# Repeated columns in the gate products and row statistics carried from one stage into the next norm

## The reference

```
def _layernorm(x, axis=-1, eps=1e-05):
    m = jnp.mean(x, axis=axis, keepdims=True)
    v = jnp.var(x, axis=axis, keepdims=True)
    return (x - m) / jnp.sqrt(v + eps)

x = x + _L0_xattn_ref(_layernorm(x), ctx, ctx, ...)        # cross attention
x = x + _L0_attn_ref(_layernorm(x), ...)                   # token mixing
x = x + _L0_ffn_ref(_layernorm(x), gate_w, gate_b, ...)    # feed forward
...                                                        # layers 1 to 3 alike

gate_scores = jnp.einsum('bsd,de->bse', x, gate_w) + gate_b   # in the mixtures of experts
topk_val, topk_idx = lax.top_k(gate_scores, TOP_K)
```

## Time and profile before

| | us |
|---|---|
| median of 3 runs | 3088.95 |
| lowest, highest | 3085.35, 3089.32 |
| the profiled execution | 3088.85 |
| its span | 3087.0 |

### The profile page before, as it was taken

How to read it: one execution, slowest core, us unless ns; L and a number is a source line. 1 busy time by engine, 2 the same in 40 slices (tenths; PEclk the granted TensorE clock), 3 DMA queues, 4 the chain that set the end, 5 groups by cost and what they waited for, 6 DMA issues and landing times. The chain is left out here.

```text
span 3087.0 us, 102826 instructions
## 1 busy us (share of the span) xinstructions
PE 2499.1 (81%) x30020; PEld 1971.3 (64%) x30021; DVE 2154.2 (70%) x7789; ACT 1872.6 (61%) x5990; POOL 1776.9 (58%) x1942
## 2 busy tenths in 40 slices
PE   4964799489999879888999983489669999979571
PEld 2843687367777678766777761477547777758561
DVE  5978422478888868727888887632279999979525
ACT  3841444379999723347999975144358888847320
POOL 1832477367777664025777762057547777749271
PEclk9985899799999989889999996589889999989685
DMA  2002455311111030003333320135534544500132
GB/s 103 3 1 99 128 154 153 98 45 41 39 39 39 27 130 0 0 1 76 79 79 79 81 46 0 66 117 153 147 82 116 115 118 114 116 5 3 57 106 67
DMA packets 195910, 225.58 MB, mean 73 GB/s; under 512 B 24899, under 2 KB 166211, under 8 KB 194724
## 3 DMA queue, kind: packets, MB, share of 16 engines
q1 hardware_dynamic: 183076, 197.57, 24.3%
q0 software_dynamic: 12672, 25.98, 3.1%
HBM read 201.69 MB, written 21.76 MB: 72 GB/s over the span
## 5 line engine op out<-in xcount | busy, mean ns | idle before, releaser
L1803 POOL TENSOR_TENSOR sx<-sx,rs 128x1028 f32<-128x1028 f32 x384 | 731.3, 1904 | 280.4 <-DVE rs L1951 280.2
L1896 ACT ACTIVATE sx<-sx,nm 128x257 f32<-128x257 f32 x1536 | 771.1, 506 | 115.8 <-DVE nm L1939 115.8
L1939 DVE CUSTOM_DVE_ANT_0 sx<-bank,rows 128x257 f32<-128x257 f32 x1024 | 411.1, 421 | 50.8 <-PE bank L1886 48.5
L1606 ACT ACTIVATE hT<-bank,B 128x128 f32<-128x128 f32 x714 | 205.7, 367 | 279.6 <-PE bank L1574 277.8
L350 POOL TENSOR_TENSOR rstd<-var,nhalf 128x8 f32<-128x8 f32 x48 | 79.1, 1648 | 414.0 <-DVE var L381 414.0
L1896 ACT ACTIVATION_READ_ACCUMULATOR sx<-sx,nm 128x1 f32 x1536 | 290.9, 189 | 0.0
L1886 PE MATMUL bank<-kT,qb 32*128 32x257 f32 x3072 | 278.6, 428 | 0.0
L1958 DVE COPY pt<-bank 128x512 f32<-128x512 f32 x384 | 263.8, 687 | 2.0 <-PE bank L1821 1.7
L1821 PE MATMUL bank<-C,sx 128*128 128x128 f32 x1536 | 251.6, 286 | 2.8 <-POOL sx L1803 2.7
L1840 PEld LDWEIGHTS bank<-W,ct 128*128 128x128 f32 x1536 | 219.5, 192 | 52.1 <-DVE nm L1939 18.1
L1870 PE MATMUL bank<-pt,vs 128*32 128x128 f32 x6144 | 245.6, 277 | 4.7 <-ACT pt L1905 4.6
(11 more groups left out here) (391 smaller groups left out, 5629.4 us busy)
## 6 DMA issues: line engine op xcount, KB each, us to landing
ct<-in_ctxT SPq DMA_DIRECT2D x384, 128.5 KB
W<-in_L_w SPq DMA_DIRECT2D x159, 256.0 KB
rows<-rows_x SPq DMA_DIRECT2D x256, 128.5 KB
keep<-rows_keep SPq DMA_DIRECT2D x128, 128.5 KB
yg<-copy_outs SPq DMA_DIRECT2D x40, 256.0 KB
token_rows<-XN SPq DMA_DIRECT2D x24, 256.0 KB, 2.3
W<-in_L_w SPq DMA_DIRECT2D x1, 6144.0 KB, 16.9
W<-in_L_w SPq DMA_DIRECT2D x39, 128.0 KB
```

Source lines behind the costliest of these rows:

```text
L1803: pool.tensor_tensor(sx[:, j, :, 0:KEYS], sx[:, j, :, 0:KEYS], rs[:, j, :].unsqueeze(2).to_broadcast([P, 4, KEYS]), ALU.mult).then_inc(p_r ...
L1896: ins = act.activation(sx[:, j, h, 0:KEYS], sx[:, j, h, 0:KEYS], ACT.Exp, bias=nm[:, j, h:h + 1], scale=-1.0, accum_out=sm[:, j, h:h + 1])
L1939: dve.tensor_tensor_reduce(sx[:, j, h, 0:KEYS], B[h][:, 0:KEYS], add, -1.0, 3.0e38, ALU.add, ALU.min, nm[:, j, h:h + 1]).then_inc(s_summed ...
```

## The change

Four things are changed.

1. In the norms of the three mixtures the gate weights are streamed through each tile several times in one product: `gw` is broadcast along a new dimension of `wide` copies, so that a product has 128 columns (E = 8) or 120 (E = 24, and 96, 72, 48 at the end of a bank). The copies land in the columns behind the tile's own and are overwritten by the next tiles' products. Bank 4 now holds 20 tiles, bank 5 has 12.
2. Two cross attentions (x1, x2) and the butterfly's experts measure X's tiles as they add to them, in pairs: DVE `measure` (`bn_stats`), `gather_pair` (two `bn_aggr`), `keep_pair` (two `tensor_scalar`), POOL `root_pair` and `shift_pair`. 30 tiles are carried out of a cross attention, 28 out of the experts; the norm that follows (attn8's, rglru's, x2's) measures the rest.
3. Which engine normalises and which copies a group is given by strings, one letter a group. With carried statistics ACT and DVE alternate, DVE first (rglru: DVE alone). DVE now normalises with `rstd` and `nmr` and so waits for `stat_ready` in place of `rstd_ready`, in every norm. The norms of the two 16-head attentions give DVE one group in place of two, or seven to ACT in place of six.
4. The cross attentions' loop is written out for 16 slots before it loops, all three of them.

```
-                                h, j = t // (TILES // 2), t % (TILES // 2)
-                                pe.matmul(B[4 + h][:, j * E:(j + 1) * E], XNT[:, t * P:(t + 1) * P], gw, start=True, stop=True)
+                                h, j = (0, t) if t < GATE_TILES else (1, t - GATE_TILES)
+                                wide = min(P // E, 512 // E - j)
+                                pe.matmul(B[4 + h][:, j * E:(j + wide) * E].rearrange("p (r e) -> p r e", e=E), XNT[:, t * P:(t + 1) * P],
+                                          gw.unsqueeze(1).to_broadcast([P, wide, E]), start=True, stop=True)
...
+        def measure(dve, rows, tile, slot):
+            if not isinstance(tile, int):
+                dve.sem_inc(sig.sems["dve_passed"], 1)
+            dve.bn_stats(pair_st[:, slot:slot + 1, :], X[:, bass.ds(tile, 1), :]).then_inc(rows.measured.sem, 1)
+        def gather_pair(dve, rows, tile):
+            dve.wait_ge(*rows.measured(tile + 2))
...
+            dve.bn_aggr(pair_mv[:, 0, :], pair_st[:, 0, :]).then_inc(rows.gathered.sem, 1)
+            dve.bn_aggr(pair_mv[:, 1, :], pair_st[:, 1, :]).then_inc(rows.gathered.sem, 1)
+        def keep_pair(dve, rows, tile):
+            dve.wait_ge(*rows.gathered(tile + 2))
+            dve.tensor_scalar(mean[:, bass.ds(tile, 2)], pair_mv[:, :, 0], -1.0, None, ALU.mult)
+            dve.tensor_scalar(var[:, bass.ds(tile, 2)], pair_mv[:, :, 1], EPS, None, ALU.add).then_inc(rows.var_ready.sem, 1)
+        def root_pair(pool, rows, tile, pair):
+            pool.wait_ge(*rows.var_ready(pair + 1))
+            pool.tensor_tensor(rstd[:, bass.ds(tile, 2)], var[:, bass.ds(tile, 2)], nhalf[:, 0:2], ALU.pow).then_inc(rows.rstd_ready.sem, 1)
+        def shift_pair(pool, rows, tile, pair):
+            pool.wait_ge(*rows.rstd_ready(pair + 1))
+            pool.tensor_tensor(nmr[:, bass.ds(tile, 2)], mean[:, bass.ds(tile, 2)], rstd[:, bass.ds(tile, 2)], ALU.mult)\
+                .then_inc(rows.stat_ready.sem, 1)
...
-                NA = (5, 6, 5, 6)[len(jobs)] if len(gates) < 2 else 2
+                if st_rows.carried:
+                    by_act = ("DADADADA", "DADADADA", "DADDADDA", "DADAADAA")[len(jobs)] if len(gates) < 2 else "DDDDDDDD"
+                else:
+                    by_act = ("AAAAADDD", "AAAAAADD", "AAAAADDD", "AAAAAADD")[len(jobs)] if len(gates) < 2 else "AADDDDDD"
...
+                        if next_rows.carried and r_ % 4 == 0 and ok(x - 12):
+                            tl = (x - 12) // 4 if isinstance(x, int) else i * (U // 4) + (r_ - 12) // 4
+                            if not (isinstance(x, int) and tl >= next_rows.carried):
+                                dve.wait_ge(*x_added(tl + 1))
+                                measure(dve, next_rows, tl, (r_ - 12) // 4 % 2)
+                        tile0 = (x - 17) // 4 if isinstance(x, int) else i * (U // 4) - 4
+                        if next_rows.carried and r_ == 1 and x_past(x, 17):
+                            gather_pair(dve, next_rows, tile0)
+                        if next_rows.carried and r_ == 2 and x_past(x, 17):
+                            keep_pair(dve, next_rows, tile0)
...
+                            for t in range(GT * (g - 1), GT * g) if g else ():
+                                dve.wait_ge(*x_added(g))
+                                measure(dve, next_rows, t, t % 2)
...
-                    for x in range(U):
-                        stages(x, x, 0, lambda b: 0 <= b < N)
-                    with (steps.loop(1, N // U, per) if steps else eng.Fori(1, N // U)) as i:
+                    for x in range(2 * U):
+                        stages(x, x % U, x // U, lambda b: 0 <= b < N)
+                    with eng.Fori(2, N // U) as i:
...
+        rows_x1, rows_a1 = Rows(0), Rows(TILES - 2)
+        xattn(rows_x1, rows_a1, "x1")
```

More of the change, by code:

```diff
@@ L28 @@
 GW = GT * P
+GATE_TILES = 5 * GT
 GROUPS = TILES // GT
@@ L303, in _, with __init__, before @@
                 st_.close()
-        def norm(add_back=False, XN=None, fetch=None, jobs=(), gates=(), loading=False, logits=None):
-            with ExitStack() as c2:
-                QT = TILES // 4
-                NA = (5, 6, 5, 6)[len(jobs)] if len(gates) < 2 else 2
-                NC = NA if not jobs else GROUPS
+        class Rows:
+            def __init__(self, carried):
+                self.carried = carried
+                self.first = carried // 2
+                self.rest = [(carried, TILES)] if carried else [(q * TILES // 4, (q + 1) * TILES // 4) for q in range(4)]
+                self.parts = [(2 * k, 2 * k + 2) for k in range(self.first)] + self.rest
+                self.measured, self.gathered = sig("tile_measured", carried), sig("tile_gathered", carried)
+                self.var_ready, self.rstd_ready, self.stat_ready = \
+                    (sig(n, len(self.parts)) for n in ("var_ready", "rstd_ready", "stat_ready"))
+            def before(self, tile):
+                return next(k for k, (a, b) in enumerate(self.parts) if a <= tile < b) + 1
@@ L312, in norm @@
                 NP = 2 if jobs else 4
[L313 removed]
+                order = list(range(GROUPS)) if jobs or gates or st_rows.carried else [0, 1, 2, 5, 3, 6, 4, 7]
                 st = hold(c2, "stats", [P, TILES, 6])
[L315 to L316 removed]
+                dif = hold(c2, "dif", [P, TILES])
                 xn = hold(c2, "xn", [P, TILES, P]) if XN is None else XN
[L318 removed]
@@ L346, in _ @@
                 def _(pool):
[L347 to L352, removed]
+                    for q, (a, b) in enumerate(st_rows.rest):
+                        k = st_rows.first + q
+                        pool.wait_ge(*st_rows.var_ready(k + 1))
+                        pool.tensor_tensor(rstd[:, a:b], var[:, a:b], nhalf[:, 0:b - a], ALU.pow).then_inc(st_rows.rstd_ready.sem, 1)
+                        pool.wait_ge(*st_rows.rstd_ready(k + 1))
+                        pool.tensor_tensor(nmr[:, a:b], mean[:, a:b], rstd[:, a:b], ALU.mult).then_inc(st_rows.stat_ready.sem, 1)
                     if add_back:
@@ L381, in _, with normed @@
                         dve.scalar_tensor_tensor(out=var[:, qs], in0=var[:, qs], scalar=1.0 / P, in1=dif[:, qs],
-                                                 op0=ALU.mult, op1=ALU.add).then_inc(var_ready.sem, 1)
+                                                 op0=ALU.mult, op1=ALU.add).then_inc(st_rows.var_ready.sem, 1)
+                    def normed(g):
+                        dve.wait_ge(*st_rows.stat_ready(st_rows.before(g * GT + GT - 1)))
+                        for t in range(g * GT, (g + 1) * GT):
+                            ins = dve.tensor_scalar(xn[:, t, :], X[:, t, :], rstd[:, t:t + 1], nmr[:, t:t + 1], ALU.mult, ALU.add)
+                            if t < g * GT + GT - 1:
+                                st_.count(ins)
+                        ins.then_inc(xd_ready.sem, 1)
                     def turned(g):
@@ L386, in turned, with evict @@
                         dve.tensor_copy(XNT[:, g * GW:(g + 1) * GW], B[at % NP][:]).then_inc(xnT_dve.sem, 1)
[L388 to L399, removed]
+                    def evict(k):
                         for j in (0, 2):
@@ L405, in _ @@
                                                   ALU.add, ALU.mult).then_inc(done[j].sem, 1)
-                    for g in range(NC if jobs else NC + 1, GROUPS):
-                        turned(g)
+                    normed_here, turned_here = ([g for g in range(GROUPS) if by[g] == "D"] for by in (by_act, turned_by))
+                    if st_rows.carried:
+                        for k in range(GROUPS + 2):
+                            if k in normed_here:
+                                normed(k)
+                            if k - 1 in turned_here:
+                                turned(k - 1)
+                            if 0 <= k - 2:
+                                evict(k - 2)
+                    else:
+                        for k in range(GROUPS):
+                            if k == 2 and not jobs:
+                                turned(turned_here[0])
+                            for g in normed_here[k:k + 1]:
+                                normed(g)
+                            evict(k)
+                        for g in turned_here[1:]:
+                            turned(g)
                     st_.close()
@@ L963, in _ @@
                             pool.tensor_tensor(yg, yg, base.unsqueeze(1).to_broadcast([P, GT, P]), ALU.add).then_inc(x_based.sem, 1)
+                        for k in range(next_rows.first):
+                            root_pair(pool, next_rows, 2 * k, k)
+                            shift_pair(pool, next_rows, 2 * k, k)
                 def over_experts(eng, body):
@@ L1751, in run, with x_past @@
                         stages(x, x % U, x // U, lambda b: 0 <= b < N)
+                def x_past(x, first):
+                    return not isinstance(x, int) or x >= first
                 @block.sync
```

121 lines of the change are left out of this document (74 added, 47 removed).

## The result

The changed kernel takes 3058.36 us (median of 4 runs, 3056.95 to 3061.74) against 3088.51 (4 runs): 0.9907 of the time before, 95% interval 0.9893 to 0.9921, so some 30 us less by the medians. Two executions further down, one of unroll_only (5214 us) and one of x3_carried (11040 us), were far slower than all others of the same kernel and are in no ratio.

What follows compares the result with a forecast made beforehand. No single bound; PE paces the cross attentions and sits at half clock in gate norms. −12.0 − 3.8 − 3.7 + 0 + 0.5 + 4.5 − 1.0 = −15.5 from 3088.85: 3073.4 us, range 3064 to 3086.

Steps and rivals of the forecast that it cites:

- Gate products, −12.0: Norms of the three mixtures: 128-column products raise PE's clock, gaining 4.0 us a norm, −12.0 over three.
- 1.16 for the products: Gate norms at the high clock: a group's eight product records take 1.16 us, 1.6 us with the transposes.
- So 0.67 costs 0.13, and I take 0.15 a pair: +4.5: Loops with pairs: four small DVE operations, 0.67 us, lengthen the turn; 0.15 us a pair over 30 pairs, +4.5.
- The stage behind is PE's and moves with it: attn8, behind its norm: paced by PE, it shifts with the norm's start, 3.4 to 3.8 us earlier, −3.8 taken.
- clock early, loop for nothing: Better case for the whole kernel: clock rises early, the loop's additions are free, time under 3064 us; chance 0.05.
- Statistics carried, −3.8 and −3.7: Norms of attn8 and rglru: carried statistics give earlier starts, −3.8 and −3.7 us; x2's norm 0, between −2 and +4.
- The waits for the shift, +0.5: Other norms (x1, x3, rwkv): DVE waits for the shift instead of the root, 0 to 0.3 us each, +0.5.
- Unrolling, −1.0: Three cross attention loops: 16 unrolled slots save one turn of the loop each, −1.0 us (0 to −1.6).
- (a): Rival: the loops pay 0.4 us a pair in place of 0.15, +7.5 us, time 3081 us; chance 0.15.
- (c): Rival: DVE's additions break the loop's rhythm, 1.0 us a pair, +30 in place of +4.5, 3099 us; chance 0.05.
- (b): Rival: the clock doesn't rise in the gate norms, +6.6 us in place of −12, time 3092 us; chance 0.10.
- the prediction's estimate by it, 6.4 us a norm: Gate norms: by the skill page's N ÷ 1.2 GHz, wider products cost 6.4 us more a norm; the trace says 2.2.

Runs made afterwards that it cites:

- unroll_only: The kernel before with 16 slots written out in the three cross attentions, nothing else: 3087.44 us, 1.0002 of the time before.
- x3_carried: The changed kernel with statistics also carried out of the third cross attention, 30 tiles, into the last 16-head attention's norm: 3058.24 us, 0.9908.
- carried_only: The changed kernel with the gate products and bank split of the kernel before: 3072.32 us, 0.9960 of the time before.
- gates_only: The kernel before with only the gate products' repeated columns and the new bank split: 3071.24 us, 0.9952 of the time before.
- combined: The changed kernel with attn8's butterfly-weight transfers late, POOL's additions after DVE's normalisation in the 24-expert norm, x3 at 8 slots: 3057.23 us, 0.9902.

## Why the prediction was wrong

**Gate products, −12.0; measured −15.** The mechanism was right: the clock rises 4.0 to 6.5 us after the first transpose in all three norms. The step that failed is the pace behind the rise, "1.16 for the products". 1.16 is the duration of a merged row from first start to last end; from start to start eight records take 0.89, and a group 1.33 in place of 1.6. Over some five steps that is 1.4 us a norm. In layer 3 the rise also came at 4.0 us where 6.34 was taken, which is worth some 0.7 more: from the first transpose to the last product's end it is 13.6 us there and 14.3 in layer 2, where the rise came at 6.5. Layer 0 gained 2, not 4, for the reason that the prediction gave and priced too low.

**"So 0.67 costs 0.13, and I take 0.15 a pair: +4.5"; measured 0.** The turn is 26.53 and 26.66 as before. I carried x3's sensitivity over to loops in which PE shows no wait for `a`. X3's own turn with pairs, +0.36, shows that there is a price there, over twice the 0.15.

**"The stage behind is PE's and moves with it"; measured −5.5 in attn8.** This is the step that put the time outside the range: with the gates' 3 us and the pairs' 4.5 put right, the forecast would be 3065.9, inside it, and with attn8's 5.5 it is 3060.4. The case that the prediction gave 0.05, "clock early, loop for nothing", had two of the three. Some 1.4 us are in the norm itself: ACT and DVE alternate, so that the first three groups are transposed in 2.82 us, and the last transpose starts 7.8 us after the first, not 9.2. The other 4 are behind it and have nothing to do with the statistics: unroll_only alone gives them. Most of what unroll_only saves there, 3.4 of 4.2, is waits of PE without a releaser in straight-line code, each ending shortly behind a packet of instructions; the rest, and the division in the changed kernel, stay open. The view of idle time had the long wait in plain sight, 4.57 without a releaser; I looked at the norms only.

**Statistics carried, −3.8 and −3.7; measured −3.9 and −3.9** from the addition to the first transpose, x2's norm −0.5 where I took 0. **The waits for the shift, +0.5**: 0.25 in x1's and x3's norm (12.67 to 12.92 from first to last transpose) and 1.2 in layer 0's, seen in carried_only. **Unrolling, −1.0**: rather +0.9 to +1.9 a loop where it stands alone.

The measured terms are −15 for the gates, −8.3 for the three starts and −5.5 for attn8, −28.8 together; the rest (the butterfly's chance, x3's +1.1, layer 0's wait) is within what the stretches vary by themselves. Of the rivals (a) and (c) fall with the turn, (b) with the granted clock of 0.84. The Trainium skill's page "TensorE: Matmul & The Clock Gate", section "What's actually happening", has the throttle as a default that activity releases; that the kernel before stayed throttled with PE busy all the time and this one doesn't, at the same count of products, is what the runs add. Of its start to start for warm products of 128 columns, 55.6 ns (section "Wait — 56ns, not 53.3ns?"), the trace has twice as much, 0.111 us, for each of the two records of a 32-bit product. That section also has a start to start that never drops below some 25 ns however few the columns, so the prediction's estimate by it, 6.4 us a norm, would be 5.2; the sum didn't use it.

## What to carry to other kernels

Work put on an engine that waits for the pace-setting one can be free, as in x1 and x2; its idle time in the turn as a whole doesn't tell (x3). Read the idle time ahead of the very instructions it stands in front of, and whether the pace-setting engine waits for what is pushed behind it. A pace is read from start to start, never from a merged row's duration. And code that got longer moved the places at which later straight-line code waited without a releaser: look for such waits in the stages behind a change.

## What was not expected of the hardware

- PE waited up to 4.86 us in attn8 (gates_only) for what I read as its own program: 16 KB packets on an instruction queue came 6.9 to 7.0 us apart beside 9.7 MB of transfers (1100.61, 1107.63, 1114.51 before), 4.6 to 7.0 apart with these held back.
- DVE's normalisation of four tiles took 4.93 us beside POOL's additions (changed kernel) and 1.10 with these held back (combined). A tile of that group takes 1.27 to 1.30, where one takes 0.34 alone, as long as one of POOL's additions (1.26), and ends just behind one; POOL's additions are no longer than without DVE (1.26 to 1.28 in both). The Trainium skill's page "SBUF — State Buffer", section "Who interferes with whom", has DVE and POOL share one pair of ports by an exclusive lock, and the trace agrees with that.
- The same loop body took 26.53 us a turn in one program and 26.64 in another that differed in the slots written out ahead of it.
